# A condition-mixed FFN with routed LoRA: three column groups of 388, 388 and 384 become 512, 512 and 136

## The reference, cut to what matters

```python
# x: (128, 64, 1024), cond: (128, 128)
att   = softmax(mlp(cond))                                  # (128, 8)
agg_w = einsum('bk,koi->boi', att, weight)                  # a 64x64 mixing matrix per sample
y     = einsum('boi,bih->boh', agg_w, x) + (att @ bias_k)[:, :, None]
base   = y @ base_W.T                                       # 1024 -> 1024
logits = y @ router_W.T                                     # 1024 -> 8 experts
w_dense = top-2 of softmax(logits), renormalised            # (.., 8)
mid = einsum('bsd,edr->bser', y, lora_A) * w_dense          # 1024 -> 8*16, scaled per expert
out = x + base + 2 * einsum('bser,erd->bsd', mid, lora_B)   # 128 -> 1024
```

## Time and profile before

| | |
|---|---|
| three executions, median | 1074.57 us (1072.95 to 1074.8) |
| span of the profiled execution (first to last instruction) | 1071.6 us |
| PE busy | 1049.3 us (98%), 6386 matmuls |
| PEld busy | 1045.9 us (98%), 6386 loads |
| DVE / ACT / POOL busy | 443.8 / 142.0 / 18.8 us |
| mean granted clock of TensorE | 0.997 |

### The profile page before, as it was taken

The page is one execution under the profiler, slowest core; times in us unless marked ns, Lnnn a source line. Parts: engine busy times, 40 slices in busy tenths (PEclk is TensorE's granted clock), DMA queues, the critical chain, the costliest instruction groups (busy, mean ns, idle before and its releaser), DMA issues.

```text
span 1071.6 us, 17561 instructions
## 1 busy us (share of the span) xinstructions
PE 1049.3 (98%) x6386; PEld 1045.9 (98%) x6386; DVE 443.8 (41%) x1317; ACT 142.0 (13%) x310; POOL 18.8 (2%) x19
## 2 busy tenths in 40 slices
PE   4899999999999999999999999999999999999998
PEld 3899999999999999999999999999999999999998
DVE  3543443433433433434434434434444444344344
ACT  4511111111111111111111111111111111111110
POOL 4200000000000000000000000000000000000000
PEclk9899999999999999999999999999999999999999
DMA  8512122122122122122122122122122122122211
GB/s 188 131 44 86 44 87 85 44 86 85 43 86 86 43 86 86 43 86 86 43 86 86 45 83 86 46 83 86 47 82 86 48 80 86 56 73 86 64 43 59
DMA packets 48895, 79.64 MB, mean 74 GB/s; under 512 B 22472, under 2 KB 31432, under 8 KB 48848
## 3 DMA queue, kind: packets, MB, share of 16 engines
q1 hardware_dynamic: 39376, 45.87, 16.1%
q10 hardware_dynamic: 9504, 33.56, 7.9%
HBM read 43.76 MB, written 33.59 MB: 72 GB/s over the span
## 4 chain that ended last, share of the span: by engine, by line
PE 96%; DMA 1%; DVE 1%; ACT 1%; SPq 0%; issue 0%; DVEq 0%
PE acc L389 76%; PE y_ps L364 11%; PE acc L413 8%; DMA x_sb<-in_L_cond_weight 1%; PE y_ps L398 1%; PE acc L291 0%; ACT agg L179 0%; DVE mixk L594 0%; ACT w_hi L470 0%; DVE w_lo L570 0%; PE y_ps L308 0%; DVE out_sb L693 0%; ACT mixk L485 0%; PE acc L343 0%; SPq L199 0%
## 5 line engine op out<-in xcount | busy, mean ns | idle before, releaser
L389 PE MATMUL acc<-w_hi,y_hi 128*128 128x388 f32 (+1 forms) x1536 | 395.2, 363 | 0.7 <-DVE y_lo L635 0.7
L389 PE MATMUL acc<-w_hi,y_lo 128*128 128x388 f32 (+1 forms) x1536 | 356.2, 338 | 0.0
L389 PE MATMUL acc<-w_lo,y_hi 128*128 128x388 f32 (+1 forms) x1536 | 356.1, 338 | 0.0
L389 PEld LDWEIGHTS acc<-w_lo,y_hi 128*128 128x128 f32 x1536 | 277.3, 188 | 0.0
L389 PEld LDWEIGHTS acc<-w_hi,y_lo 128*128 128x128 f32 x1536 | 276.2, 188 | 0.0
L389 PEld LDWEIGHTS acc<-w_hi,y_hi 128*128 128x128 f32 x1536 | 247.4, 190 | 1.0 <-issue 0.9
L364 PE MATMUL y_ps<-mix_w,x_sb 128*128 128x128 f32 x1024 | 196.2, 275 | 0.0
L364 PEld LDWEIGHTS y_ps<-mix_w,x_sb 128*128 128x128 f32 x1024 | 186.1, 190 | 0.0
L640 DVE COPY logits<-acc 128x8 f32<-128x8 f32 x64 | 10.7, 167 | 296.1 <-PE acc L389 296.1
L627 DVE TENSOR_TENSOR y_sum<-y_ps,bias_sb 128x512 f32<-128x512 f32 x128 | 88.4, 691 | 77.6 <-PE y_ps L364 77.6
L635 DVE TENSOR_TENSOR y_lo<-y_sum,y_hi 128x512 fp32r<-128x512 f32 x128 | 87.9, 686 | 45.4 <-ACT y_hi L519 45.4
(11 more groups left out here) (75 smaller groups left out, 283.6 us busy)
## 6 DMA issues: line engine op xcount, KB each, us to landing
x_sb<-in_x SPq DMA_DIRECT2D x64, 512.0 KB, 4.7
out<-out_sb ACTq DMA_DIRECT2D x63, 512.0 KB, 4.9
w_stage<-in_L_ffn_base_W SPq DMA_DIRECT2D x8, 512.0 KB, 15.3
bias_sb<-bias_rows SPq DMA_DIRECT2D x64, 64.0 KB, 3.6
mix_w<-agg SPq DMA_DIRECT2D x126, 16.0 KB, 4.2
x_sb<-in_L_cond_weight SPq DMA_DIRECT2D x4, 128.0 KB
la_raw<-in_L_ffn_lora_A SPq DMA_DIRECT2D x8, 64.0 KB, 3.4
out_sb<-in_L_ffn_lora_B SPq DMA_DIRECT2D x1, 512.0 KB, 4.7
```

Source lines behind the costliest of these rows:

```text
L389: last = nc.tensor.matmul(acc[s][g][:, 0:z - a], y[:, s, c * P:(c + 1) * P], w[:, c, a:z], start=(c == 0 and first), stop=(c == NC - 1 and ...
```

## The change

The three groups become columns 0 to 512, 512 to 1024 and 1024 to 1160. Base fills two whole banks, and the third bank holds only the LoRA and router columns (SIDE = 0). `up` now has two groups, since the third holds no base column. `add_x` adds two groups, and every count of finished groups goes by UP = 2 in place of 3. Operand data, terms and their order over the groups are as before.

```diff
-    GW = -(-NW // 3 // 4) * 4
-    GROUPS = [(0, GW), (GW, 2 * GW), (2 * GW, NW)]
-    SIDE = D - 2 * GW
+    GROUPS = [(0, D // 2), (D // 2, D), (D, NW)]
+    SIDE = 0
+    UP = 2
...
             def load(t, k):
 
-                sp.wait_ge(out_ready, 3 * (t - XR) + 3)
+                sp.wait_ge(out_ready, UP * (t - XR) + UP)
...
-                    pe.wait_ge(out_ready, 3 * (t - 2) + 3)
+                    pe.wait_ge(out_ready, UP * (t - 2) + UP)
                 last = main_products(k, c, range(3))
...
-                for g in range(3):
+                for g in range(UP):
                     up_group(k, g)
 
             def up_group(k, g):
-                a, z = GROUPS[g][0], min(GROUPS[g][1], D)
+                a, z = GROUPS[g]
...
-                for g in (2, 1, 0):
+                for g in (1, 0):
                     up_group(k, g)
...
-            for n, g in enumerate((2, 1, 0)):
-                a, z = GROUPS[g][0], min(GROUPS[g][1], D)
-                act.wait_ge(out_ready, 3 * (NT - 1) + n + 1)
+            for n, g in enumerate((1, 0)):
+                a, z = GROUPS[g]
+                act.wait_ge(out_ready, UP * (NT - 1) + n + 1)
...
-            def add_x(t, k, groups=(0, 1, 2)):
+            def add_x(t, k, groups=(0, 1)):
...
-                    a, z = GROUPS[g][0], min(GROUPS[g][1], D)
-                    dve.wait_ge(up_done, 3 * t + n + 1)
+                    a, z = GROUPS[g]
+                    dve.wait_ge(up_done, UP * t + n + 1)
```

More of the change, by code:

```diff
@@ L529, in split_mid @@
                 if from_tile(t, 1):
-                    act.wait_ge(up_done, 3 * t)
+                    act.wait_ge(up_done, UP * t)
                 nc.scalar.activation(mid_hi[:, :], mid_ps, ACT.Copy).then_inc(mid_hi_ready, 1)
@@ L549, in store @@
             def store(t, k):
-                act.wait_ge(out_ready, 3 * t + 3)
+                act.wait_ge(out_ready, UP * t + UP)
                 act.dma_start(out_t[t, :, :], out_sb[:, k % 2, :]).then_inc(out_stored[k % 2], 16)
@@ L554, in _ @@
             split_mid(NT - 1, (NT - 1) % XR)
-            for n, g in enumerate((2, 1, 0)):
-                a, z = GROUPS[g][0], min(GROUPS[g][1], D)
-                act.wait_ge(out_ready, 3 * (NT - 1) + n + 1)
+            for n, g in enumerate((1, 0)):
+                a, z = GROUPS[g]
+                act.wait_ge(out_ready, UP * (NT - 1) + n + 1)
                 act.dma_start(out_t[NT - 1, :, a:z], out_sb[:, (NT - 1) % 2, a:z]).then_inc(out_stored[1], 16)
             act.wait_ge(out_stored[0], 16 * (NT // 2))
-            act.wait_ge(out_stored[1], 16 * (NT // 2 - 1 + 3))
+            act.wait_ge(out_stored[1], 16 * (NT // 2 - 1 + UP))
         @block.vector
@@ L722, in _ @@
             split_mid(*last)
-            add_x(*last, groups=(2, 1, 0))
+            add_x(*last, groups=(1, 0))
     return nc
```

## The result

The changed kernel takes 1143.69 us (median of 4 executions, 1143.29 to 1143.88) against 1073.99 us for the kernel before beside it: ratio 1.0649, 95% interval 1.0634 to 1.0664. It is 6.5% slower. The forecast was 1143 us.

What follows compares the result with a forecast made beforehand. PE was taken as the bound, through the distances between its matmul starts. Triples +69.1, up -1.2 and the last add +0.1 gave +68.0 us: span 1139.6, plus 3.0 around it, 1143 us, 6.3% slower; 90% range 1131 to 1157.

Steps and rivals of the forecast that it cites:

- The bound: Whole kernel: PE is busy 1049.3 of 1071.6 us, so distances between matmul starts go into the time one for one.
- The floor: Main product: a 136-column matmul costs 113 ns (109 to 118), set by the weight load, not its 57 ns stream.
- The rival that the long streams hide the load: Main product: weights fetched two matmuls ahead, a short matmul costs 72 ns, time about 1073 us; chance 4%.
- Two of the three observations: Evidence for the floor: line 308's 111 to 114 ns, line 343's 110 ns, fp32r load records of 188 against 142 ns.
- Line 343's 110 ns at clock 0.50: Line 343: seven matmuls streaming 8 columns still start 110 ns apart, taken as a sign of the load's floor.
- the longer record of the fp32r load: PE's weight loads: 188 ns for an fp32r block against 142 ns before a transpose, so the load has a length.
- The wide matmul: Main product and up: a 512-column matmul takes 231 ns, the middle of 228.6 (fixed overhead) and 233.6 (proportional).
- A triple: Main product, one term's three matmuls: from 530 to 575 ns, 1536 times, +69.1 us (bounds +55.6 to +84.8).
- `up` with its six wide matmuls: up, each tile: 1404 ns becomes 1386, over 64 tiles -1.2 us (bounds -2.1 to -0.1).
- DVE's adds: add_x: two adds of some 700 ns replace three, 0.13 us a tile less, costed at nothing; DVE busy about 8 us less.
- The last tile's cover: Last tile: 12 short matmuls, 1.36 us where there were 2.1, must cover the split of `mid`; it fits.
- what lies around the span: Outside the profile's span: 3.0 us from 1071.6 us up to the median of 1074.57, said not to change.

Runs made afterwards that it cites:

- the sweep: Kernel before plus twelve fp32r matmuls per width, 8 to 512 columns, after PE's last matmul; 112 ns apart at 8 to 128 columns, 63 ns for 136 with half the load.
- the padded kernel: Changed kernel with the third group widened from 136 to 232 columns by computing 96 base columns again: 1143.35 us, ratio 1.0646 to the kernel before.
- the split kernel: Changed kernel with up's second bank written in pieces of 264 and 248 columns, nine matmuls a tile again: 1143.07 us, ratio 1.0643 to the kernel before.

## Why the prediction was right

**The bound.** PE alone sets the time, and the distances between its starts add up. Confirmed: no new wait inside the tiles (what is new, 0.8 us for the first tile's mixing weights and 0.3 us at line 308, lies before them), and 1.08 us a tile explain 69.1 of 70.6 us.

**The floor.** It was predicted from 128 and 248 columns as 109 to 118 ns, with 113 taken. Measured: 112 in the last tile, 111 by leaving the short matmuls out, and the sweep, where the load's width moved it, shows its cause, which line 308 had only suggested. The rival that the long streams hide the load is refuted by the loads themselves, since that of a short matmul's successor never starts before the short matmul, though 512 columns stream ahead of it, and by the padded kernel. The Trainium skill's figure ("TensorE: Matmul & The Clock Gate", LDWEIGHTS), columns / 1.2 or 107 ns for 128, is near the 112 here. For 32 and 64 loaded columns no floor shows above 63 ns, which is also what the rule asks. It isn't the whole of it: the rule has no clock in it, and at clock 0.50 the fp32r load's floor was 213 ns.

Two of the three observations that the prediction gave for the floor don't carry it. Line 343's 110 ns at clock 0.50 were taken for the same floor, but at that clock the fp32r floor is 213. In the changed kernel's profile line 343 ran at clock 1.00 (its timeline of PE, and the window's granted clock):

```profile
38.14 0.66 PE L343 MATMUL acc<-ident,out_sb 8*128 8x8 f32 x8
```

```profile
37.00:38.80 1.80, 1.80 (x19) 1.54 (x18) 1.72 (x4) 1.70 (x5) 1.72 (x2) 1.00 0.01 1
```

One of the eight lasts 0.20 us, so they stand (0.66 - 0.20)/7 = 65 ns apart, where the sweep's fp32r matmuls with as few columns stand 112. Line 343 transposes a block of only 8 rows; it is another case, and that its 110 at half clock came near 112 is chance. Nor does the longer record of the fp32r load mean a higher floor. In the kernel before, line 291's transposes had these loads from 30.1 to 36.5 us, at clock 1.00:

```profile
L291 PEld LDWEIGHTS acc<-ident,w_stage 128*128 128x128 f32 x24 | 2.6, 144 | 0.3 <-issue 0.2
```

Read one by one, these matmuls stand 109 ns apart with loads of 144 ns, the fp32r ones 112 with loads of 188. What carried the 113 was line 308, and the 248-column row as its upper bound.

**The wide matmul.** 231 ns was taken from between 228.6 and 233.6; measured are 232, in the tiles, in `up` and in the sweep, where no DMA and no other engine ran. So the excess over 2.4 GHz doesn't come from the DMAs or from the other engines. It is 14 ns at 388 and 19 at 512 columns, nearly proportional, but not in line between (16 ns at 344, 14 at 448); where it comes from stays open, and the middle value of 231 was a guess that came out. The Trainium skill's rule ("TensorE: Matmul & The Clock Gate", Back-to-back issue gap), N/2.4 + 2.5 ns or 216 ns for 512, doesn't hold for these fp32r streams.

**The terms.** A triple measured 576 ns (575 taken); `up` with its six wide matmuls gave nothing that the split kernel could show (1.2 us taken); DVE's adds last 692 ns (700) and its busy time fell by 3.6 us, not 8, because the prediction counted every add at its full length, 1.53 us for the three, where they overlap and take 1.42; it cost nothing either way. The last tile's cover held: the split of `mid` ended in time, and PE shows no wait.

**What was wrong.** Besides line 343 three smaller things, none worth more than 3 us. First, "the matmul after each 136-column one starts 109 to 118 ns after it" is not what the trace writes: it is recorded after 63 ns and waits within its record; only its load shows the 109. Second, what lies around the span was taken as 3.0 us, from a median and another execution's span; for the profiled execution of the changed kernel it is 1143.88 - 1142.2 = 1.7, and executions of the kernel before, each against its own span, give 1.9. The rest of the 3.0 was the difference between executions. Third, the span grew by 70.6 us, not 68.0: 1.2 us of that are in the tiles (a triple is 1 ns longer than taken), the rest lies around them. In that profile the clock of the prologue stood at 0.50 until later, into the first tile. The windows of the changed kernel, early:

```profile
44.00:49.00 5.00, 5.00 (x15) 4.23 (x16) 1.11 (x2) 0.63 (x1) 0.00 (x0) 0.50 0.69 223
50.00:60.00 10.00, 10.00 (x59) 8.65 (x57) 1.39 (x2) 0.64 (x1) 0.00 (x0) 1.00 0.01 2
```

The kernel before stood at clock 1.00 from 44 to 49 us. Those 5 us at half clock are worth up to 2.5 us. Against them stands that the clock also fell later, being 1.00 from 37 to 38.8 us (the window above) where it was 0.50 before, and the first main matmul started 0.66 us earlier (43.96 against 44.62). That leaves up to 1.8 us, enough for the 1.5 us by which the span grew beyond the tiles. Nor need the change have caused it: the sweep, which is the kernel before up to its last tile, has clock 0.50 from 44 to 48 us as well. The second and the third thing partly cancel (1.3 us too much, 2.6 too little), which is luck.

## What to carry to other kernels

Where each matmul brings its own weight load, find the width below which the load is the longer (here an estimated 245 columns for fp32r blocks of 128x128, from 112 ns at 0.456 ns a column), and split the columns so that no group falls below it. Equal groups are the safe way, unequal ones above the floor cost the same (456, 456, 248 in the main product), and filling whole banks is worth nothing by itself. A matmul's mean duration and PE's busy share don't show this wait; the distances between starts of equal stretches, or the starts of the weight loads, do.

No version that does all the work beat the kernel before (the one without most short matmuls leaves work out). The sweep says why: its main groups lie on the straight part of the curve, where columns alone are paid, and the least of its `up` groups, 248 columns at 114 ns, sits at the corner.

## What the runs showed of the hardware beyond that

- A matmul that waits for its weights is recorded from the end of the stream before it, 63 ns behind a 136-column one, 106 ns behind a 232-column one, and its record is longer (439 ns against 397).
- At granted clock 1.00 a wide fp32r stream runs at some 0.45 to 0.46 ns a column (344: 160 ns, 388: 176, 448: 201, 512: 232), and at 388 and 512 columns this holds with all other engines idle as well as with them at work.
- A stretch of short matmuls alone, 27 of them from 1069 to 1072 us in the sweep, was followed by clock 0.50, though PE's records were busy throughout; there the floor is 213 ns. Two stretches of twelve in the last tile, between long ones, did not lower it.
- The record of a load before a transpose lasts 142 ns, that of a load before an fp32r matmul 188, and that of one of 64 columns 135. Its length says little about the floor: 109 ns for the transposes of 128x128 blocks, 112 for the fp32r matmuls.
